# Attention score maxima in paired and gathered matmuls, with single-head score banks

## The reference

```python
attn = jnp.einsum('bqhd,bkhd->bhqk', Q, K) * scale     # Q, K after RoPE
attn = jnp.where(causal, attn, NEG_INF)
attn = jax.nn.softmax(attn, axis=-1)
out = jnp.einsum('bhqk,bkhd->bqhd', attn, V).reshape(B, S, dim)
```

## Time and profile before

| | us |
|---|---|
| median of three runs | 3551.72 (3551.53 to 3552.5) |
| the profiled execution, its own time | 3548.13 |
| its span, first to last instruction | 3546.4 |
| attention stage, first GpSimd instruction to the last copy of `ps_o` | 323.8 to 2150.1 |
| one group, from the first exponent to the next group's first (750.23 to 857.61) | 107.4 |
| the next group, at whose start the loop turns back (857.61 to about 970.6) | 113.0 |

### The profile page before, as it was taken

How to read it: one execution, slowest core, us unless ns; L and a number is a source line. 1 busy time by engine, 2 the same in 40 slices (tenths; PEclk the granted TensorE clock), 3 DMA queues, 4 the chain that set the end, 5 groups by cost and what they waited for, 6 DMA issues and landing times. The chain is left out here.

```text
span 3546.4 us, 64058 instructions
## 1 busy us (share of the span) xinstructions
PE 3175.5 (90%) x18948; PEld 1799.1 (51%) x18948; DVE 2645.6 (75%) x6114; ACT 1569.4 (44%) x2096; POOL 763.4 (22%) x619
## 2 busy tenths in 40 slices
PE   5885999999999999999999996764599999799998
PEld 3552233333333333333333334554588888678787
DVE  4885888888887888878788833887477777566666
ACT  1442166666666666666566672111244444211111
POOL 1775000000000000000000002777332323333332
PEclk8997599999999999999999997665799999899999
DMA  1776111111111111111111104553554545322222
GB/s 66 190 206 192 42 31 46 45 54 47 38 39 45 54 47 42 36 45 54 47 44 35 34 7 110 171 165 121 171 163 151 162 152 163 115 89 89 89 89 71
DMA packets 372705, 315.08 MB, mean 89 GB/s; under 512 B 99436, under 2 KB 359000, under 8 KB 372440
## 3 DMA queue, kind: packets, MB, share of 16 engines
q1 hardware_dynamic: 360152, 278.26, 26.6%
q0 software_dynamic: 12288, 33.57, 2.8%
HBM read 194.27 MB, written 116.92 MB: 88 GB/s over the span
## 5 line engine op out<-in xcount | busy, mean ns | idle before, releaser
L820 ACT ACTIVATE probs<-ps_s 128x1024 f32<-128x1024 f32 (+3 forms) x1280 | 1083.5, 894 | 728.6 <-PE ps_s L957 475.1
L947 PE MATMUL ps_m<-k_st,q_st 96*128 96x512 bf16 (+3 forms) x2560 | 838.0, 363 | 47.9 <-POOL k_st L801 30.9
L957 PE MATMUL ps_s<-q_st,k_st 98*128 98x512 bf16 (+3 forms) x2560 | 714.4, 352 | 27.0 <-issue 20.3
L973 PE MATMUL ps_o<-probs,vs 128*32 128x512 f32 (+3 forms) x5120 | 605.0, 545 | 0.0
L845 DVE CUSTOM_DVE_ANT_0 masked<-ps_m,mask_qk 128x512 bf16<-128x512 f32 (+3 forms) x1024 | 462.5, 489 | 163.1 <-PE ps_m L947 150.9
L947 PEld LDWEIGHTS ps_m<-k_st,q_st 96*128 96x128 bf16 x2560 | 215.3, 97 | 715.7 <-DVE piece_late L848 205.7
L848 DVE TENSOR_REDUCE piece_late<-ps_m 128x1 f32<-128x512 f32 x768 | 473.1, 681 | 30.5 <-PE ps_m L947 29.8
L848 DVE TENSOR_REDUCE piece_rest<-ps_m 128x1 f32<-128x512 f32 x768 | 475.0, 682 | 27.5 <-PE ps_m L947 18.7
L1218 POOL MEMSET zeros<- 128x1024 f32 x1 | 1.0, 956 | 1815.1 <-POOLq L670 1815.1
L957 PEld LDWEIGHTS ps_s<-q_st,k_st 98*128 98x128 bf16 x2560 | 242.2, 98 | 247.5 <-ACT probs L820 67.7
L962 PE MATMUL ps_s<-mask_kq,ident_b 128*128 128x128 bf16 x1024 | 204.4, 219 | 0.0
(11 more groups left out here) (226 smaller groups left out, 5423.2 us busy)
## 6 DMA issues: line engine op xcount, KB each, us to landing
qk_parts<-parts SPq DMA_DIRECT2D x128, 192.0 KB, 2.9
k_st<-qk_parts SPq DMA_DIRECT2D x384, 64.0 KB, 2.3
q_st<-qk_parts SPq DMA_DIRECT2D x384, 64.0 KB, 2.3
x_r<-expert_rows SPq DMA_DIRECT2D x39, 512.0 KB, 4.5
expert_made<-made SPq DMA_DIRECT2D x39, 512.0 KB, 3.0
x_in<-in_L_attn_x_dram SPq DMA_DIRECT2D x32, 512.0 KB, 4.6
v_ones<-v_out SPq DMA_DIRECT2D x64, 256.0 KB, 4.7
vs<-v_ones SPq DMA_DIRECT2D x64, 256.0 KB, 3.6
```

The costliest lines, as they stand in the source:

```text
L820: act.activation(probs[:, u % PSLOTS, 2 * pair:2 * pair + 2, j * P:ST], ps_s[:, pair, :, j * P:ST], ACT.Exp, scale=SCALE).then_inc(exp_don ...
L947: pe.matmul(ps_m[:, bank, 0:w], q_st[0:ROWS, slot, h, qi * P:(qi + 1) * P], k_st[0:ROWS, slot, h, kt * ST:kt * ST + w], start=True, stop=T ...
L957: last = pe.matmul(ps_s[:, pair, hh, j * P:ST], k_st[0:ROWS + MROWS, slot, h, kc * P:(kc + 1) * P], q_st[0:ROWS + MROWS, slot, h, qt * ST ...
L973: last = pe.matmul(ps_o[h * VW:(h + 1) * VW, j * P:ST], vs[:, slot, kc, h * VW:(h + 1) * VW], probs[:, u % PSLOTS, h, j * P:ST], start=(kc ...
```

## The change

Four things, all in `attention_stage`:

1. **Head rows.** Odd heads lie at other rows than even ones (`HEAD_ROWS`). The three largest products (`MAIN = 3`, high x high, high x low part, low x high) are rows 0 to 47 of an even head and 64 to 111 of an odd one; the shift rows are 96 and 112. Each load is split by parity of the head: 24 DMAs for a quarter of the sequence, each with half the bytes. Odd heads' rows 0 to 15 must be zero, so VectorE (slot 0) and GpSimd (slot 1) each do one fill of ones (32 x 8192) and two of zeros (16 x 4096), and SP waits for VectorE's before its first load.
2. **Pieces become units.** A piece is now w columns wide, where w counts only keys in blocks ahead of the queries' own block; that block is a separate unit. With w = 512 or 384, two heads form a unit: two matmuls of only the 48 main rows, at row 0 and at row 64 of the array, into the two banks of one double bank. With w = 256 two heads and with w = 128 four are gathered side by side in one bank, with all rows. The diagonal blocks of four heads are gathered too (4 x 128) and a matmul of the identity and `mask_qk` (512 columns) adds the mask. VectorE reduces every unit with one plain maximum that gives two or four columns of results. `ps_m` is two double banks instead of three banks.
3. **Single-head score banks.** `ps_s` has three banks, one head each, used in turn. ScalarE's exponent is one instruction per head. TensorE at position u does: score of u head 3, of u+1 head 0, units, head 1, units, head 2, values of u.
4. **Plan.** `plan_of` gives units to 80 half-positions in proportion to columns, not in proportion to number.

```diff
+MAIN = 3
+HEAD_ROWS = ((0, 16, 32, 48, 64, 80), (64, 80, 96, 16, 32, 48))
+SHIFT_ROW = (96, 112)
+MAX_BASE = (0, 64)
...
-            now = spread[a:b]
...
+            out[min(m for m in range(1, 2 * NPOS) if at[m] * total >= past * at[2 * NPOS - 1])].append(unit)
...
-        ps_s = ps("ps_s", [P, 2, 2, ST])
-        ps_m = ps("ps_m", [P, BANKS, ST])
+        ps_s = ps("ps_s", [P, SBANKS, ST])
+        ps_m = ps("ps_m", [P, BANKS, 2, ST])
...
-                        act.activation(probs[:, u % PSLOTS, 2 * pair:2 * pair + 2, j * P:ST],
-                                       ps_s[:, pair, :, j * P:ST], ACT.Exp, scale=SCALE).then_inc(exp_done, 1)
+                        act.activation(probs[:, u % PSLOTS, h, j * P:ST], ps_s[:, (HG * u + h) % SBANKS, j * P:ST],
+                                       ACT.Exp, scale=SCALE).then_inc(exp_done, 1)
...
-                    stand_alone(v, held)
-                    v.tensor_tensor_reduce(masked[:, bank, 0:w], ps_m[:, bank, 0:w], mask_qk[:, ST - w:ST], 1.0, LOWEST,
-                                           ALU.add, ALU.max, dst).then_inc(m_taken, 1)
-                else:
-                    v.tensor_reduce(dst, ps_m[:, bank, 0:w], AX.X, ALU.max).then_inc(m_taken, 1)
+                v.tensor_reduce(dst, src, AX.X, ALU.max).then_inc(m_taken, 1)
...
+                for second, (qi, col, k0, w, h, n) in enumerate(unit):
+                    for i in range(n):
+                        z, a = (h + i) % 2, (h + i) // 2
+                        rows = slice(MAX_BASE[z], MAX_BASE[z] + MAIN * HD) if n == 1 else slice(0, SHIFT_ROW[z])
+                        last = pe.matmul(ps_m[:, bank, second, i * w:(i + 1) * w],
+                                         q_st[rows, slot, z, a, qi * P:(qi + 1) * P], k_st[rows, slot, z, a, k0:k0 + w],
+                                         start=(i == 0), stop=(i == n - 1 and k0 != qi * P), skip_group_check=True)
+                    if k0 == qi * P:
+                        last = pe.matmul(ps_m[:, bank, 0, :], ident_b[:, :],
+                                         mask_qk[:, :, :].rearrange("p h t -> p (h t)"),
+                                         start=False, stop=True, skip_group_check=True)
...
+                for u in range(NPOS):
+                    score(g, u, par, HG - 1)
+                    next_score(u, 0)
+                    some(todo[2 * u])
+                    next_score(u, 1)
+                    some(todo[2 * u + 1])
+                    next_score(u, 2)
                     values(g, u, par)
```

More of the change, by code:

```diff
@@ L624, in plan_of, with work @@
+    def work(unit):
+        return sum((what.w * what.n if isinstance(what, Piece) else P) + P for what in unit)
     def plan_of(first, maxima):
-        spread = with_late(PIECES) if maxima else []
-        out = []
+        spread = with_late() if maxima else []
+        out = [[] for _ in range(2 * NPOS)]
+        width = [ST - P * max(0, kc - TPS * qt) + P for qt, kc in POSITIONS]
+        at = [0]
         for u in range(NPOS):
-            a, b = (len(spread) * (u - 1) // (NPOS - 1), len(spread) * u // (NPOS - 1)) if u else (0, 0)
-            now = spread[a:b]
[L632 to L638, removed]
+            at += [at[-1] + width[(u + 1) % NPOS], at[-1] + width[(u + 1) % NPOS] + width[u]]
+        total, past = sum(work(unit) for unit in spread), 0
+        out[1].append(["turn rest"])
+        for unit in spread:
+            out[min(m for m in range(1, 2 * NPOS) if at[m] * total >= past * at[2 * NPOS - 1])].append(unit)
+            past += work(unit)
+        if not first:
+            out[7].append([("turn o", -1, NQ - 1)])
+        for k, u in enumerate(LAST_OF[:-1]):
+            out[2 * (u + 2) + 1].append([("turn o", 0, k)])
@@ L877, in divide, with item @@
                 v.sem_inc(m_taken, 1)
-            def item(what, g, gm, count, bank, stored):
+            def item(unit, g, gm, count, bank, stored):
+                what = unit[0]
                 if what == "turn rest":
@@ L939, in item, with score @@
                     turn_max(gm, 0, bank)
[L940 removed]
+                elif isinstance(what, Piece):
+                    pieces(unit, bank, slot, turn)
+                else:
                     turn_o(g + what[1], what[2], bank)
[L942 to L950 removed]
+            def score(g, u, slot, h):
                 qt, kc = POSITIONS[u]
@@ L1005, in _ @@
                 if idx >= BANKS:
                     pe.wait_ge(m_taken, idx - BANKS + 1)
-                item(what, 0, 0, idx % BANKS, 0, 1)
+                item(unit, 0, 0, idx % BANKS, 0, 1)
             pe.wait_ge(max_in[0][0], 16 * MAX_DMAS)
-            for pair in range(2):
-                scores(0, 0, 0, pair)
+            for h in range(HG - 1):
+                score(0, 0, 0, h)
             body(0, 0, True, FIRST_PLAN, size(PROLOGUE), True)
```

216 lines of the change are left out of this document (120 added, 96 removed).

## The result

The changed kernel takes 3742.3 us (3740.6 to 3745.0), the kernel before 3551.6 us: a ratio of 1.0546, interval 1.0532 to 1.0559. It is 191 us slower; forecast were 131 slower, at 3683. The profiled execution's span went from 3546.4 to 3738.8 us.

What follows compares the result with a forecast made beforehand. The prediction took TensorE to bound the kernel. Its terms, 54 (TensorE's work) + 30 (banks) + 27 (loop turns) + 8 (last group) + 12 (start) = +131 us on 3548.1, gave 3679 profiled, 3683 median; range 3500 to 3745.

Steps and rivals of the forecast that it cites:

- side by side: The two matmuls of a 64-row pair on TensorE run together, costing one matmul plus the second's start, taken as 0.02 us.
- the price of shape: TensorE's changes of tile shape around pairs: 0.093 us going in, 0.10 going out, 10.4 us per group.
- A full position: TensorE has no wait left in its 2.83 us; a lone pair then costs 0.43 us, as two pieces did before.
- rivals with free changes of shape: Going to 64-row tiles costs TensorE nothing: 3460 to 3544 us (chance 0.17), or 3545 to 3600 if other engines close in (0.15).
- pairs not side by side: On TensorE each pair's second half waits for the first: 10.8 us more a group, +162, 3845 us; chance 0.06.
- TensorE's own work: TensorE's matmuls and shape changes per group: +3.6 us (-6.8 to +8), +54 in the 15 groups with pieces.
- the term for banks: Units waiting for double banks still held by VectorE's reductions: +2 us per group (0 to +4), +30 in all.
- The 3.7: TensorE's waits per group before the change, in us: summed work of 103.7 against a length of 107.4.
- The 5.5: Bank waits per group after the change, in us: 18 places with two units in one half-position, at 0.3 each.
- the loop turns: ScalarE's loop, now 374 instructions, loses 3 to 4 us per turn; 3 shows at nine turns: +27 us (0 to +40).
- start and last group: Fills and loads delay the first score, +12 us (+3 to +15); exponents without units between lengthen the last group, +8.
- the range's upper end for the shape change: TensorE's work at its dearest: +8 us per group, with 0.058 us for a pair's second start and 0.146 going out.

## Why the prediction came out as it did

**Right: side by side, and the price of shape.** A full position was forecast at no gain, and has none, 2.83 us. The entry is 0.10 us where 0.093 was taken from the values, the exit 0.10 as chosen. The rule of the Trainium skill that changing the tiling mode drains TensorE (TensorEngine Tiling (Array Packing), Key Properties) agrees with these two steps in that both are longer; how far the array drains they do not say, since the next matmul starts after 0.33 us, ahead of the 0.39 at which the profile lets the one before end. The rivals with free changes of shape fall with them, and so does that of pairs not side by side. Two sizes were off and cancel in part: by the starts of single matmuls in the trace the second half comes 3 or 4 ns after the first, not 20, and a matmul behind a change of used rows or of shape some 8 ns later than behind none. TensorE's own work grew by about 4.35 us a group, forecast 3.6, which is 11 of the missing 61 us.

**Wrong: the term for banks.** This is the step that failed. The prediction set "18 x 0.3 = 5.5 us against 3.7 of waits now" and took +2 us a group, +30 in all, with +4 as its upper end. Measured are +4.75 for banks, +0.6 for the cut of the maxima and +0.3 for ScalarE, 5.65 a group: about 82 us in the 15 groups, the first of which is 2 us cheaper. Both numbers were off.
- The 3.7 was the rest between a sum of prices and a length, and was read as waits. The run with short reductions says 2.45 for banks; the rest was in the sum.
- The 5.5 counted units behind units, at 0.2 to 0.6 us. There were twelve waits for reductions by the profile's count, fewer than 18. But four are of turns of outputs, 2.4 us of the 5.3 in the table of waits. They were not priced, since only units were looked at, and three of them are the worst placed: like the one at 809.87, they come behind two pairs whose reductions take over a microsecond each. Nor was the chain from the turn of the maxima over VectorE's cut to the next pair.

**Right in sum, wrong in its parts: the loop turns.** Forecast +27, measured +28. ScalarE does lose time at its turn, as forecast: the gap at 795.42 is 2.52 us, and 0.56 where the loop is written out. That 374 instructions are enough for it is not shown by their number alone, since VectorE's 295 lost 4.11 us in one kernel and 0.47 in the other. And what shows of ScalarE's turn in a group's length is 1.8 us on average at nine turns, 16 in all, and not 3: about 1 us where the clock stays full, and 1.6 more in the four groups where it falls, which the prediction did not have. The gap was forecast at 4 us with the word issue, and reads 2.52 with TensorE's name. The other 12 us are TensorE's second stop with the longer slow stretch behind it, which was not forecast and which padding takes away. The two misses cancel, so the sum of this term is right by luck; the group with TensorE's turn, which was to be about 119 us long, is 126.1.

**Right: start and last group.** +12.6 for +12, with the first score at 438.9 for 437. ScalarE's timeline in the last group, which answers to the earlier trace rows:

```profile
2276.46 2.06 ACT L858 ACTIVATE probs<-ps_s 128x512 f32<-128x512 f32 x4 [0.33 <-PE ps_s L1010]
2278.86 2.06 ACT L858 ACTIVATE probs<-ps_s 128x512 f32<-128x512 f32 x4 [0.33 <-PE ps_s L1010]
```

A position is 2.40 us where 2.45 was worked out and half of 4.25 was needed before. The last group is 8.9 us longer, forecast 8.

**Sum.** 52 of the missing 61 us are waits, 11 TensorE's work, 1 the loops, 1.5 start and last group, and the rest of the program gave 4 back. The result stands at the very end of the range: 3742.3 as measured, about 3745.5 by the ratio to the kernel before, against 3745. That it came so near is owed to the range's upper end for the shape change and not to the one for banks, which was too low.

What stays open: which of the banks' waits a different order would avoid (turns in half-positions of their own were not tried), why the clock falls in four of nine like groups, and whether the four changes pay one by one, since they were never run apart.

## What to carry to other kernels

Where small-tile matmuls stand between full ones, count the changes of shape before the saved columns: here a change in and out costs as much as a whole 512-column matmul, so a single pair gains nothing and two in a row gain 0.2 us. When banks are merged into fewer, larger ones, price every user of them that follows another, transposes and the chains behind them too, by the time from its bank's last matmul to the end of a reduction of the new size; and take the waits of now from an experiment that shortens the consumer, not from the rest of a sum. If a loop's rounds are long and few, try it written out early: here it gave 1.0 and 1.7%, and at a turn look at the granted clock too, which can stay low after the engine has started again.

## What the runs showed of the hardware

- A change from a 128 x 128 to a 64 x 128 tile and back cost about 0.10 us each way on TensorE (0.33 and 0.32 us to the next start where 0.22 is usual); 240 fewer in each direction (16 x 15) gave 49 us.
- Two 512-column matmuls on the two row tiles take 0.39 us together, as one does; their starts are 3 or 4 ns apart.
- TensorE's loop turn cost one stop (3.9 to 4.2 us before the change, 2.9 to 3.5 with the padding) or two (3.0 to 3.7 and 2.2 to 2.8 us), by where its instructions lie: 32 instructions ahead of the loop took 15 us off five turns. VectorE's unchanged loop in the middle stage lost 4.11 us at its turn in one kernel and 0.47 in the other.
- With such a stop TensorE's granted clock read 0.50 (1.2 GHz) for some 7 us with one stop (3.4 once) and 10 us with two, the end of the stop included, and the same values took 1.87 us instead of 1.00 at that level. It also read 0.50 for 3.4 us behind pauses of only 0.66 and 0.46 us, and stayed full in a like place behind pauses of 0.95 and 0.46.
- Written out, the same instructions lost nothing: the groups had one length, and the kernels took 35 and 60 us less (by the ratios). The Trainium skill, Runtime: NRT & Kernel Launch, Instruction fetch mechanics, says that a taken branch breaks the sequential prefetch and prefers unrolling; these runs agree, with 1.0% and 1.7% of the kernel before as its price.
